# Two aggregations of a graph network kernel: gathers released by the product itself, index columns copied six at a time

## The chip, the core and the metric

One core of a Trainium2 chip runs the whole program. TensorE (PE in the rows) multiplies matrices, and its weight loads stand apart as PEld; VectorE (DVE), ScalarE (ACT) and GpSimd (POOL) work element by element, and SyncE (SP) starts plain transfers. Each engine runs its own instruction stream in order. They meet through semaphores: an instruction adds to a counter when it is done, another engine's instruction waits until the counter has reached a number. A gather (rows of a table in the chip's main memory, picked by a column of indices) is a DMA that GpSimd prepares and starts; its rows land later and count up a semaphore of their own.

The metric is the device time of one execution in microseconds (us), the median of several runs.

## The reference

Four layers follow one another, each with a residual: a graph attention layer, a mixture of eight experts, a graph convolution with edge weights, and a mixture of four experts whose routing is itself a small graph attention. The change touches the two edge aggregations over the same 53125 edges and 3125 nodes, of 256 values each:

```python
# layer 0: softmax over the edges of each destination node
m = jax.ops.segment_max(a, dst, num_segments=N)
a = jnp.exp(a - m[dst])
denom = jax.ops.segment_sum(a, dst, num_segments=N)
a = a / (denom[dst] + 1e-16)
out = relu(jax.ops.segment_sum(h[src] * a[:, None], dst, num_segments=N))
# layer 2: weighted sum
gathered = A_values[:, None] * h[col]
agg = jax.ops.segment_sum(gathered, row, num_segments=A_shape)
```

## The kernel before

Nodes lie in 25 tiles of 128 (`NT`). The edges, sorted by destination, lie in columns of 128; six columns (`BG`) are a block, and the blocks of a tile are its edges. `emit_aggregate` is called twice: with tag `a0` and `softmax` true for the attention layer (its blocks start where the tile's edges start), and with tag `a1` for the convolution, where every tile's blocks are padded and lie one behind another. The number of blocks is read at run time; in this data there are 77 in `a0` (462 gathers) and 74 in `a1` (444 gathers), some three a tile.

For every column of a block four things happen:

1. ScalarE copies one column of source indices into one of six places of `idx` (`put_indices`, L572 to L574).
2. GpSimd gathers 128 rows of 260 values by them into one of six places of `rows` (L589).
3. A matrix of weights `w` (128 edges by 128 nodes, zero where edge and node don't belong together) is made: in `a0` by ScalarE as an exponential of a mask `nb` (L789), in `a1` by VectorE (L658).
4. TensorE multiplies `w` by `rows` and adds to the tile's sum in PSUM (L619). One product is two matrix instructions in the trace, since the data is float32.

The semaphore `agg_done` counts these products; PE starts it at `BG` = 6. ScalarE's copy of column i of block g waits until it reaches `g * BG + i + 1`, that is, until the product that used the same place one block earlier is done. The copy adds one to `indexed`, and the gather waits for that count. So the place in `rows` is guarded through ScalarE: product, copy, gather. In `a0` ScalarE's stream is, for each block, six copies, a wait for the mask (`masked`), and six exponentials; between tiles it reads the next tile's range (L780 to L783). In `a1` it has the copies alone.

VectorE in `a0` walks the tiles in a loop of 22 turns (the other three tiles stand before and behind it): copy the negated maxima (`keep_max`, L716), mask the first block (L722, L726), negate the next tile's maxima (L708 to L712), mask the other blocks, finish the previous tile (`finish_tile`, L734 to L740), and scan the tile two ahead for its maxima (`scan`: six masks L684 and six maxima L701 a block). The masks `nb` go into a ring of four blocks, so VectorE may run ahead of ScalarE and TensorE. In `a1` VectorE makes `w` and evicts each tile's sum (L661); at a tile's end TensorE closes the sum with a product of zeros (L623) and opens the next with another (L612).

Of the kernel before, what the change touches and what calls it, by code (L numbers as in the profile page):

```python
# [15 lines left out]
P = 128  # L16
# [486 lines left out]
def emit_aggregate(nc, S, tag, table, softmax):  # L503
# [9 lines left out]
    with ExitStack() as ctx:  # L513
        sb = lambda n, s, d: ctx.enter_context(nc.sbuf_tensor(tag + n, s, d))
        idx = sb("idx", [P, BG], I32)
# [55 lines left out]
        def put_indices(act, g, c):  # L571
            for i in range(BG):  # L572
                act.wait_ge(agg_done, g * BG + i + 1)
                nc.scalar.copy(idx[:, i:i + 1], source[:, bass.ds(c + i, 1)]).then_inc(indexed, 1)  # L574

        @block.gpsimd
        def _(pool):
            if softmax:
                total = tile_range(nc, pool, S, NT - 1)[0]
            else:  # L580
                total = pool.value_load(S.eranges[0:1, NT:NT + 1], min_val=1, max_val=EBLOCKS)
            count = pool.alloc_register(tag + "_count")
            pool.reg_mov(count, 0)
            with pool.Fori(0, total) as g:
                for i in range(BG):
                    pool.reg_add(count, count, 1)
                    pool.wait_ge(indexed, 1)
                    pool.wait_ge(indexed, count)
                    pool.indirect_dma_start(rows[:, i, 0:TW], None, table,  # L589
                                            bass.IndirectOffsetOnAxis(ap=idx[:, i:i + 1], axis=0)).then_inc(gathered[i], 16)  # L590

        @block.tensor
        def _(pe):
            pe.sem_inc(agg_done, BG)
# [50 lines left out]
        if not softmax:  # L645
            @block.vector
            def _(v):
# [3 lines left out]
                with v.Fori(0, NT) as t:  # L651
                    tiles.load(t)
                    tiles.step()
                    with tiles.blocks() as g:
                        c = tiles.chunk(g)
                        for i in range(BG):
                            v.wait_ge(agg_done, g * BG + i + 1)
                            nc.vector.tensor_scalar(w[:, i, :], S.iota[:, 0:P], S.elane[:, bass.ds(c + i, 1)],  # L658
                                                    S.eweight[:, bass.ds(c + i, 1)], ALU.is_equal, ALU.mult).then_inc(weighed, 1)
# [5 lines left out]
            def _(act):  # L665
                total = act.value_load(S.eranges[0:1, NT:NT + 1], min_val=1, max_val=EBLOCKS)
                with act.Fori(0, total) as g:
                    put_indices(act, g, slot_of(nc, act, g, EBLOCKS, BG))
            return
# [106 lines left out]
        def _(act):  # L776
# [3 lines left out]
            with act.Fori(0, NT) as t:  # L780
                tiles.load(t)
                tiles.step()
                with tiles.blocks() as g:  # L783
# [3 lines left out]
                    for i in range(BG):  # L787
                        act.wait_ge(agg_done, g * BG + i + 1)
                        nc.scalar.activation(w[:, i, :], nb[:, bass.ds(g % RING, 1), i, :].rearrange("p a n -> p (a n)"), ACT.Exp, bias=S.score[:, bass.ds(c + i, 1)]).then_inc(weighed, 1)  # L789

# [1050 lines left out]
```

## Time and profile before

| | before |
|---|---|
| median of 3 runs | 3885.39 us |
| lowest and highest | 3881.91 and 3893.16 us |
| the profiled execution | 3854.0 us |
| its span, first to last instruction | 3851.9 us |
| mean granted TensorE clock over the span | 0.712 |
| PE, PEld busy | 2660.5 us (69%), 1816.4 us (47%) |
| DVE, ACT, POOL busy | 1510.2 us (39%), 759.3 us (20%), 1889.8 us (49%) |
| first aggregation (`a0`), from first index copy to last sum | 704 to 1515 us |
| second aggregation (`a1`) | 2452 to 3112 us |

The table and the rows below come from one profiled execution. Busy time is that of the instructions themselves: a wait, a register instruction or the flight of a DMA is not in it. A row of a timeline has the start, the length, the engine, the line, the operation with what it writes and reads, the number of instructions merged into it, and in brackets how long the engine had been idle and what the profile takes for the releaser. "issue" there means that no semaphore ended the idle time: the engine's own sequencer was late.

### The profile page before, as it was taken

How to read it: one execution, taken by the hardware profiler on the slowest of the kernel's cores; microseconds unless marked ns; L12 is line 12 of the kernel's file. 1: busy time of each engine (PE TensorE's matmuls, PEld its weight loads, DVE VectorE, ACT ScalarE, POOL GpSimd, SP SyncE). 2: the span in 40 equal slices, each digit the busy share in tenths (PEclk: the TensorE clock that was granted, in tenths of full speed). 3: DMA queues.
4: the chain of work that ended last, by engine and by line, in shares of the span. 5: the costliest groups of instructions: out<-in, count | busy, mean ns of one | idle time of the engine just before them, and what ended most of it. 6: DMA issues, size and time to landing. Idle time of an engine off the chain costs nothing. (4 is left out here: it accounts for less than half of the span.)

```text
span 3851.9 us, 46754 instructions
## 1 busy us (share of the span) xinstructions
PE 2660.5 (69%) x10550; PEld 1816.4 (47%) x10551; DVE 1510.2 (39%) x3666; ACT 759.3 (20%) x2605; POOL 1889.8 (49%) x1926
## 2 busy tenths in 40 slices
PE   3249688465566556699999997677777755989900
PEld 2225587233333333576767665333333334666600
DVE  5774555656666653322222223322222233000075
ACT  0136000123322222222222221111111112222200
POOL 0000666265656554366666663366666611666602
PEclk9555555566666665799999998666666665999955
DMA  2012344132222222100000000233333311110001
GB/s 73 27 38 66 143 146 147 33 83 75 79 79 79 74 76 61 33 11 12 12 12 12 14 1 20 77 91 91 91 89 92 89 26 34 20 20 8 9 36 36
DMA packets 124782, 213.24 MB, mean 55 GB/s; under 512 B 56098, under 2 KB 82807, under 8 KB 122423
## 3 DMA queue, kind: packets, MB, share of 16 engines
q0 software_dynamic: 75808, 125.28, 13.1%
q1 hardware_dynamic: 48918, 87.37, 6.7%
q8 instruction: 18, 0.29, 0.0%
q14 instruction: 38, 0.30, 0.0%
HBM read 196.99 MB, written 15.52 MB: 55 GB/s over the span
## 5 line engine op out<-in xcount | busy, mean ns | idle before, releaser
L589 POOL DMA_INDIRECT a0rows<-table,a0idx x462 | 466.3, 1009 | 363.0 <-ACT a0idx L574 250.5
L589 POOL DMA_INDIRECT a1rows<-table,a1idx x444 | 420.1, 946 | 315.3 <-ACT a1idx L574 176.6
L619 PE MATMUL a1ps<-a1rows,a1w 128*128 128x256 f32 x888 | 435.5, 616 | 173.2 <-DMA a1rows<-table,a1idx 115.9
L619 PE MATMUL a0ps<-a0rows,a0w 128*128 128x257 f32 x924 | 428.3, 602 | 153.6 <-ACT a0w L789 71.4
L1053 POOL DMA_INDIRECT erecords<-k_rece x416 | 404.5, 972 | 213.3 <-issue 103.2
L881 PE MATMUL f0up<-k_xnT,f0w 128*128 x1280 | 386.0, 457 | 59.4 <-ACT f0hid L913 33.7
L1053 POOL DMA_INDIRECT records<-k_recg x288 | 301.0, 1045 | 226.1 <-POOLq L959 74.2
L1373 POOL DMA_INDIRECT gt_land<-table_gat,gt_source x281 | 265.9, 946 | 287.7 <-DVEq L1402 141.7
L619 PEld LDWEIGHTS a1ps<-a1rows,a1w 128*128 128x128 f32 x888 | 215.5, 284 | 393.2 <-issue 278.2
L619 PEld LDWEIGHTS a0ps<-a0rows,a0w 128*128 128x128 f32 x924 | 233.5, 286 | 345.8 <-issue 176.6
L891 PE MATMUL f0dn<-f0w,f0hid 128*128 128x256 f32 x1600 | 357.6, 380 | 9.2 <-issue 8.6
L881 PEld LDWEIGHTS f0up<-k_xnT,f0w 128*128 128x128 f32 x1280 | 246.5, 199 | 193.3 <-issue 57.7
L891 PEld LDWEIGHTS f0dn<-f0w,f0hid 128*128 128x128 f32 x1600 | 304.1, 190 | 56.2 <-issue 14.6
L832 DVE SCALAR_TENSOR_TENSOR k_x<-f0dn,k_gate,k_x 128x256 f32 (+1 forms) x200 | 88.9, 479 | 507.5 <-PE f0dn L891 330.1
L913 ACT ACTIVATE f0hid<-f0up,f0b1now 128x384 f32<-128x384 f32 (+1 forms) x320 | 167.7, 528 | 539.8 <-PE f0up L881 327.8
L658 DVE TENSOR_SCALAR a1w<-k_iota,k_elane,k_eweight 128x128 f32<-128x128 f32 x444 | 148.1, 370 | 266.1 <-PE a1ps L619 149.5
L1610 PE MATMUL f1dn<-gt_arena 128*128 128x256 f32 x800 | 191.0, 388 | 28.6 <-issue 24.3
L1600 PE MATMUL f1up<-k_xnT,gt_arena 128*128 x640 | 187.5, 449 | 23.5 <-DVE gt_arena L1417 14.1
L574 ACT COPY a1idx<-k_esource 128x1 int32 x444 | 82.7, 191 | 578.5 <-PE a1ps L619 351.8
L789 ACT ACTIVATE a0w<-a0nb,k_score 128x128 f32 x462 | 143.7, 389 | 235.1 <-DVE a0nb L726 183.0
L471 PEld LDWEIGHTS es_ps<-k_we_attn,es_ea 128*128 128x128 f32 x832 | 182.1, 332 | 5.6 <-issue 5.3
L1610 PEld LDWEIGHTS f1dn<-gt_arena 128*128 128x128 f32 x800 | 152.8, 193 | 62.1 <-issue 42.3
(387 smaller groups left out, 3133.3 us busy)
## 6 DMA issues: line engine op xcount, KB each, us to landing
es_ea<-in_eaT SPq DMA_DIRECT2D x16, 1664.0 KB
es_lane<-lane_row SPq DMA_DIRECT2D x16, 832.0 KB
so_rowl<-glane_row SPq DMA_DIRECT2D x32, 256.0 KB
a0rows<-table,a0idx POOLq DMA_INDIRECT x462
a1rows<-table,a1idx POOLq DMA_INDIRECT x444
erecords<-k_rece POOLq DMA_INDIRECT x416
table<-k_tbl SPq DMA_DIRECT2D x10, 650.0 KB, 3.6
records<-k_recg POOLq DMA_INDIRECT x288
```

The costliest lines, as they stand in the source:

```text
L471: nc.tensor.matmul(ps[i][:, 2, c:c + 1], ea[:, i, c * P:(c + 1) * P], S.we_attn[:, 0:1], start=True, stop=True).then_inc(step, 1)
L589: pool.indirect_dma_start(rows[:, i, 0:TW], None, table, bass.IndirectOffsetOnAxis(ap=idx[:, i:i + 1], axis=0)).then_inc(gathered[i], 16)
L619: nc.tensor.matmul(sum_of(t), w[:, i, :], rows[:, i, 0:width], start=False, stop=False).then_inc(agg_done, 1)
L658: nc.vector.tensor_scalar(w[:, i, :], S.iota[:, 0:P], S.elane[:, bass.ds(c + i, 1)], S.eweight[:, bass.ds(c + i, 1)], ALU.is_equal, ALU.mu ...
L789: nc.scalar.activation(w[:, i, :], nb[:, bass.ds(g % RING, 1), i, :].rearrange("p a n -> p (a n)"), ACT.Exp, bias=S.score[:, bass.ds(c + i ...
L881: ins = nc.tensor.matmul(up[q % 2][:, 0:size], w1[:, k, m * P:(m + 1) * P], S.xnT[:, k, bass.ds(g * (U * P) + a * P, size)], start=(k == 0 ...
L891: ins = nc.tensor.matmul(down[j][:, 0:D], hid[half][:, k, (j - a) * P:(j - a + 1) * P], w2[:, k, :], start=(k == 0), stop=(k == KH - 1))
L913: nc.scalar.activation(hid[half][:, m, :], up[q % 2][:, 0:(b - a) * P], ACT.Gelu, bias=bias_now[:, m:m + 1]).then_inc(hid_ready, 1)
L1053: pool.indirect_dma_start(self.rec_dram, bass.IndirectOffsetOnAxis(ap=self.rec[:, c + 1, 0:1], axis=0), self.rec[:, c + 1, 1:R], None).the ...
L1373: pool.indirect_dma_start(land[:, j, :], None, S.table_gat, bass.IndirectOffsetOnAxis(ap=source[:, j:j + 1], axis=0)).then_inc(gathered[la ...
L1600: ins = nc.tensor.matmul(up[q % 2][:, 0:size], w1[:, k, m * P:(m + 1) * P], S.xnT[:, k, bass.ds(g * (U * P) + a * P, size)], start=(k == 0 ...
L1610: ins = nc.tensor.matmul(down[j][:, 0:D], hid[half][:, k, (j - a) * P:(j - a + 1) * P], w2[:, k, :], start=(k == 0), stop=(k == KH - 1))
```

## The change

The copy takes six index columns in one instruction and puts them into one of two places, by the parity of the block. It waits until `agg_done` reaches `g * BG + 1`; since the counter is now started at `BG + 1`, this means that all products of block g - 2 are done, whose gathers used the same place. `indexed` now counts blocks. The gather waits once a block for the index columns, and for each column for `agg_done` itself. GpSimd's loop goes in pairs of blocks, so that each half has its place of `idx` written in; with an odd number of blocks six gathers too many are made at the end, whose rows nobody uses, and a wait behind the loop lets all gathers land. ScalarE adds one to `indexed` at its end, for that last half pair. The waits of `w` are the same as before, written with the new start of the counter.

```diff
-        idx = sb("idx", [P, BG], I32)
+        idx = sb("idx", [P, 2 * BG], I32)
...
         def put_indices(act, g, c):
-            for i in range(BG):
-                act.wait_ge(agg_done, g * BG + i + 1)
-                nc.scalar.copy(idx[:, i:i + 1], source[:, bass.ds(c + i, 1)]).then_inc(indexed, 1)
+            act.wait_ge(agg_done, g * BG + 1)
+            nc.scalar.copy(idx[:, bass.ds(g % 2 * BG, BG)], source[:, bass.ds(c, BG)]).then_inc(indexed, 1)
...
-            count = pool.alloc_register(tag + "_count")
-            pool.reg_mov(count, 0)
-            with pool.Fori(0, total) as g:
+            pairs = pool.snap((pool.snap(total) + 1) // 2)
+            count, block_count = pool.alloc_register(tag + "_count"), pool.alloc_register(tag + "_blocks")
+            pool.reg_mov(count, 1)
+            pool.reg_mov(block_count, 0)
+
+            def gather_block(half):
+                pool.reg_add(block_count, block_count, 1)
+                pool.wait_ge(indexed, 1)
+                pool.wait_ge(indexed, block_count)
                 for i in range(BG):
                     pool.reg_add(count, count, 1)
-                    pool.wait_ge(indexed, 1)
-                    pool.wait_ge(indexed, count)
+                    pool.wait_ge(agg_done, 1)
+                    pool.wait_ge(agg_done, count)
                     pool.indirect_dma_start(rows[:, i, 0:TW], None, table,
-                                            bass.IndirectOffsetOnAxis(ap=idx[:, i:i + 1], axis=0)).then_inc(gathered[i], 16)
+                                            bass.IndirectOffsetOnAxis(ap=idx[:, half * BG + i:half * BG + i + 1], axis=0)
+                                            ).then_inc(gathered[i], 16)
+
+            with pool.Fori(0, pairs):
+                for half in range(2):
+                    gather_block(half)
+            landed = pool.snap(pairs * 32)
+            for i in range(BG):
+                pool.wait_ge(gathered[i], 16)
+                pool.wait_ge(gathered[i], landed)
...
-            pe.sem_inc(agg_done, BG)
+            pe.sem_inc(agg_done, BG + 1)
...
-                            v.wait_ge(agg_done, g * BG + i + 1)
+                            v.wait_ge(agg_done, g * BG + i + 2)
...
-                        act.wait_ge(agg_done, g * BG + i + 1)
+                        act.wait_ge(agg_done, g * BG + i + 2)
```

On ScalarE, in the loop of the second aggregation, the names are the index places (`a1idx`) and the source columns of the padded blocks (`k_esource`). Before, a turn of the loop was:

```order
L574 ISA
L574 COPY a1idx<-k_esource 128x1
L573 REGISTER_ALU
L574 ISA
L574 COPY a1idx<-k_esource 128x1
L573 REGISTER_ALU
```

and so on, six copies in all. Now the whole turn is:

```order
L681 ISA
L573 ISA
L573 COPY a1idx<-k_esource 128x6
L681 REGISTER_ALU
L681 COMPARE_AND_BRANCH
```

Five copies of six with their waits and counters are gone, and nothing else stands there. In the first aggregation the six exponentials, which stood behind the sixth copy of their block, now stand behind the one copy.

On GpSimd, in the loop of the second aggregation, the gather writes `a1rows` from `table`. Before, a block was six times this pair:

```order
L584 UNCONDITIONAL_BRANCH
L586 REGISTER_ALU
L589 DMA a1rows<-table,a1idx 128x260
L586 REGISTER_ALU
L589 DMA a1rows<-table,a1idx 128x260
```

Now the first gather of a block has one more counter ahead of it:

```order
L598 UNCONDITIONAL_BRANCH
L587 REGISTER_ALU
L591 REGISTER_ALU
L594 DMA a1rows<-table,a1idx 128x260
L591 REGISTER_ALU
L594 DMA a1rows<-table,a1idx 128x260
```

The turn has twelve gathers in place of six, and one register instruction more for each block.

## Rows read from the trace of the kernel before

**Rows 1.** The page's groups: line, engine, operation, count, busy us, mean ns, idle before.

```profile
L589 POOL DMA_INDIRECT a0rows<-table,a0idx x462 | 466.3, 1009 | 363.0 <-ACT a0idx L574 250.5
L589 POOL DMA_INDIRECT a1rows<-table,a1idx x444 | 420.1, 946 | 315.3 <-ACT a1idx L574 176.6
```

**Rows 2.** Busy time by stretch, one per aggregation: PE, PEld, DVE, ACT, POOL, clock, DMA.

```profile
704.00:1516.00 812.00, 492.52 (x1099) 269.91 (x1099) 473.58 (x1328) 228.28 (x924) 466.26 (x462) 0.62 0.28 76
2451.00:3112.00 661.00, 485.22 (x988) 243.81 (x988) 158.66 (x469) 82.69 (x444) 420.15 (x444) 0.61 0.33 90
```

**Rows 3.** Waits of VectorE, 740 to 1500 us: total us, times, longest.

```profile
DVE a0mb L684 <- issue: 102.6, 141, 4.7
DVE a0top L701 <- issue: 52.2, 60, 2.5
```

**Rows 4.** Waits of GpSimd, 740 to 1500 us.

```profile
POOL a0rows L589 <- ACT a0idx L574: 197.1, 102, 8.8
POOL a0rows L589 <- issue: 109.5, 348, 1.8
```

**Rows 5.** Waits of GpSimd, 2455 to 3105 us.

```profile
POOL a1rows L589 <- issue: 138.7, 382, 2.7
POOL a1rows L589 <- ACT a1idx L574: 92.6, 61, 3.6
```

**Rows 6.** Timeline of one tile of the first aggregation.

```profile
1026.59 0.99 POOL L589 DMA_INDIRECT a0rows<-table,a0idx  x1 [0.30 <-ACT a0idx L574]
...
1030.63 1.26 DVE L684 TENSOR_SCALAR a0mb<-k_iota,k_dstf 128x128 f32 x6 [0.51 <-issue]
...
1034.62 0.19 ACT L574 COPY a0idx<-k_src 128x1 int32 x1 [1.58 <-issue]
1034.68 0.90 DVE L684 TENSOR_SCALAR a0mb<-k_iota,k_dstf 128x128 f32 x4 [0.73 <-issue]
...
1037.95 0.95 POOL L589 DMA_INDIRECT a0rows<-table,a0idx  x1 [0.30 <-issue]
...
1040.74 1.64 DVE L701 SCALAR_TENSOR_TENSOR a0top<-a0mb,k_score,a0top 128x128 f32<-128x128 f32 x5 [1.05 <-issue]
...
1041.02 1.08 ACT L574 COPY a0idx<-k_src 128x1 int32 x6 [4.23 <-PE a0ps L619]
...
1041.98 0.95 POOL L589 DMA_INDIRECT a0rows<-table,a0idx  x1 [3.08 <-ACT a0idx L574]
...
1043.08 1.27 DVE L684 TENSOR_SCALAR a0mb<-k_iota,k_dstf 128x128 f32 x6 [0.70 <-issue]
```

**Rows 7.** Timeline around two restarts of the gathers, second aggregation.

```profile
2470.62 0.94 POOL L589 DMA_INDIRECT a1rows<-table,a1idx  x1 [0.30 <-issue]
...
2474.25 0.52 ACT L574 COPY a1idx<-k_esource 128x1 int32 x3 [4.71 <-PE a1ps L619]
2474.30 0.95 DVE L658 TENSOR_SCALAR a1w<-k_iota,k_elane,k_eweight 128x128 f32<-128x128 f32 x3 [4.55 <-PE a1ps L619]
...
2475.21 0.94 POOL L589 DMA_INDIRECT a1rows<-table,a1idx  x1 [3.65 <-ACT a1idx L574]
...
2478.09 2.46 PE L619 MATMUL a1ps<-a1rows,a1w 128*128 128x256 f32 x4 [3.95 <-DMA a1rows<-table,a1idx]
...
2719.18 1.21 PE L619 MATMUL a1ps<-a1rows,a1w 128*128 128x256 f32 x2 [0.75 <-issue]
...
2720.50 0.19 ACT L574 COPY a1idx<-k_esource 128x1 int32 x1 [1.78 <-PE a1ps L619]
...
2725.14 0.19 ACT L574 COPY a1idx<-k_esource 128x1 int32 x1 [4.44 <-PE a1ps L619]
...
2726.20 0.94 POOL L589 DMA_INDIRECT a1rows<-table,a1idx  x1 [2.19 <-issue]
```

**Rows 8.** Timeline of the end of the first aggregation.

```profile
1474.12 1.57 POOL L589 DMA_INDIRECT a0rows<-table,a0idx  x1 [2.15 <-ACT a0idx L574]
...
1492.10 0.94 POOL L589 DMA_INDIRECT a0rows<-table,a0idx  x1 [2.32 <-ACT a0idx L574]
...
1505.84 0.94 POOL L589 DMA_INDIRECT a0rows<-table,a0idx  x1 [0.30 <-issue]
...
1509.57 2.55 PE L619 MATMUL a0ps<-a0rows,a0w 128*128 128x257 f32 x4 [0.48 <-DMA a0rows<-table,a0idx]
...
1514.35 0.42 DVE L740 TENSOR_TENSOR k_x<-k_x,a0relu 128x256 f32<-128x256 f32 x1
```

More of the change, by code:

```diff
@@ L668, in _ @@
                     put_indices(act, g, slot_of(nc, act, g, EBLOCKS, BG))
+                act.drain().then_inc(indexed, 1)
             return
@@ L787, in _ @@
                     for i in range(BG):
-                        act.wait_ge(agg_done, g * BG + i + 1)
+                        act.wait_ge(agg_done, g * BG + i + 2)
                         nc.scalar.activation(w[:, i, :], nb[:, bass.ds(g % RING, 1), i, :].rearrange("p a n -> p (a n)"), ACT.Exp, bias=S.score[:, bass.ds(c + i, 1)]).then_inc(weighed, 1)
+            act.drain().then_inc(indexed, 1)
 def wait_for_event(pool, event, up_done, down_done):
```

## The prediction

> **What bounds the kernel now.** I read the page's costliest groups first, then the waits of each engine inside the two aggregations, then their timelines. The groups [rows 1] say where the change acts: 462 and 444 gathers on GpSimd, both told to wait mostly for ScalarE's index copy. By stretch [rows 2] the first aggregation takes 812 us and the second 661 us of a span of 3851.9 us; GpSimd is busy for 466 and 420 us of them. The rest of the kernel is not touched, so all that can be won or lost lies in these 1473 us.
>
> The pitch of gathers in an unbroken run is 0.95 us plus 0.30 us between two, 1.25 us [rows 6, 7]. At that pitch 444 gathers take 555 us; the second aggregation takes 106 us more, and nearly all of that is idle time of GpSimd. Its waits [rows 5] are 138.7 + 92.6 = 231.3 us; 443 gaps of 0.30 us are 133 of them, so 98 us are real stops, and 61 stops are put down to the index copy. Here the gathers are in a closed loop: gather, its landing (2.88 us from the start of the gather at 2475.21 to the product at 2478.09 [rows 7]), product, release of the place six gathers back, gather.
>
> The first aggregation is another case. Its VectorE shows in the loop no wait for another engine, only "issue" [rows 3]: it goes from scan to mask to scan without a pause, about 30.5 us a tile, and the masks and maxima of the other engines hang on it. GpSimd's 197.1 us of waiting there [rows 4] is mostly waiting for work that VectorE has not made possible yet. Where VectorE's turn is longer than the gathers' (some 18 a tile, 23 us), a faster release of gathers gives nothing.
>
> **The restart of a gather.** Today a finished product is seen by ScalarE, which copies, and by GpSimd after that. At 2719.18 a product runs 1.21 us and ends at 2720.39; the copy starts at 2720.50, a hop of 0.11 us; the copy lasts 0.19 us. At the stop after a tile's end the copy starts at 2725.14 and the gather at 2726.20, 1.06 us later [rows 7]. Without ScalarE between them the copy's 0.19 us and one hop of 0.11 us go: 0.30 us a restart. The bounds are 0 (if the copy was not what came last) and 1.06 us (all from copy to gather). I take 0.30, since the other 0.76 us lie on GpSimd after its wait and stay.
>
> Second aggregation: 61 stops by 0.30 us is 18.3 us. In unbroken runs a release comes early enough already and nothing changes. Many of the stops are not short ones: at 2474.25 ScalarE and at 2474.30 VectorE, which wait for the same counter of products, go on together after 4.71 and 4.55 us of idle [rows 7]. The counter itself came late, not the copy. GpSimd, waiting for the counter itself, gets it no sooner; it saves the 0.30 us there and not the 3.65 us. That is why I don't count the 98 us as the gain.
>
> **The copies.** Five of six are gone, some 385 and 370 of them by 0.19 us. In the second aggregation ScalarE has nothing else to do: no gain beyond the restart. In the first one the exponentials of a block stand behind its sixth copy, which waits for the last product of the block before (copy at 1034.62 [rows 6]). They can now start product by product. That moves the last block's products of a tile about 1 us forward (the landing of its first gather decides in place of the copies), and the next tile's first product still waits for VectorE's mask: 0 us in the loop, as long as VectorE is the bound.
>
> **The tail of the first aggregation.** After VectorE's last mask the chain is gathers and products. Two stops of GpSimd there, 2.15 us at 1474.12 and 2.32 us at 1492.10 [rows 8], come from copies queued behind exponentials; less the usual 0.30 us they are 1.85 + 2.02 us. The last gather starts at 1505.84; by 2.88 us to its product, and 1.23 us for one (2.46 us for two at 2478.09 [rows 7]), the end would be at 1509.95, where the last products end at 1509.57 + 2.55 = 1512.12: 2.17 us. The most is 6.0 us, the least 2 restarts, 0.6 us; I take 4.
>
> **What is added.** 77 blocks are odd, so the first aggregation makes six gathers more, each after the last block's product in its place. The last of them starts some 0.8 us after the last product and lands 2.88 us later (3.7 us), while VectorE's finish ends at 1514.35 + 0.42, 2.65 us after it [rows 8]: 1 us more. 74 blocks are even: nothing there. GpSimd's extra counter and wait a block have no row of their own. At best they hide behind the gather that is running, as the present pair does. At worst they lengthen the gap once a block, by one more 0.30 us: 151 blocks, 45 us. I take 0, because the present gap is the same 0.30 us with a counter and two waits between any two gathers, however early they were released [rows 6, 7]. The six-column copy replaces 0.19 us by something near 0.19 us, a block ahead of need.
>
> **The sum.** 18.3 + 4 - 1 = 21 us. The profiled execution takes 3854.0 us and would take 3833. The timed median is 31.4 us above the profiled one; I carry the difference over: 3885.4 - 21 = 3864 us. The own range of this case is 3846 to 3874.
>
> **A stall that may grow or shrink.** In the first aggregation the scan of a tile's second block starts at 1034.68 and the third's at 1043.08, 8.40 us, where the first took 1034.68 - 1030.63 = 4.05 us for the same instructions [rows 6]. These 4.35 us, once a tile, fall into the last part of an unbroken run of ten gathers (1026.59 to 1037.95 and its landing) and end when the run has ended; the six gathers from 1041.98 have none beside them. The 102.6 + 52.2 us of "issue" [rows 3] hold this. I take it as a stall of VectorE's (and ScalarE's) sequencer under a long run of gathers, and don't know its cause.
>
> By the Trainium skill (NOTIFIC — the notification-queue block, section 7.1) the recording of traces always pushes back on the engines when its inner queue fills, so these stalls could be those of the recording. Then timed runs would not have them and both of the next two rivals would be void. But they would then have to be faster than the profiled one, and the three timed runs are 31 us slower; no run here settles it. The sum would be the same by either.
>
> **Rivals.**
> First, slower: the runs join. The tile's first six gathers now start 3.08 us after the last ended [rows 6], released by six copies in one row at 1041.02. If ScalarE gets through its tile change before the stall begins, they follow at 0.30 us, the run becomes 16 or more, and the third block's scan is stalled like the second: 4.35 us in up to 22 turns, 96 us on the bounding engine, less the 21: 3960 us, and 3912 for half of the turns. It turns the result slower than before by more than 0.3% from 8 turns on (33 us by 4.35). For it: the stall follows the length of a run. Against: ScalarE is stalled by the same thing (4.23 us idle ahead of 1041.02), and the counter of products comes late in it, so the run would still break.
>
> Second, much faster: the stalls grow rarer, since five copies of six with their waits, counters and increments leave the engines that are stalled. Half of 22 by 4.35 us, and half of the 98 us of stops: 97 us, 3788 us. For it: the index copies are 462 of ScalarE's 924 instructions there [rows 1, 2]. Against: VectorE's and TensorE's instructions stay, and so do the gathers.
>
> Third, no gain: the second aggregation is held by TensorE. At the lower clock a product takes 1.23 us [rows 7], hardly less than the pitch of 1.25, and the clock is 0.61 on the mean there [rows 2], so mostly 1.2 GHz; 444 products and 50 products of zeros at 1.23 us would be 608 us of the 661. Gathers that start earlier would then wait as landed rows. Only the tail is left, 3 us: 3882 us.
>
> Fourth, slower: the added wait is not hidden, 45 us less 21: 3909 us. Behind it on GpSimd stands the next gather, and behind that the product.
>
> **The chances.** Forecast 0.45, joined runs 0.14, rarer stalls 0.15, TensorE the bound 0.20, the added wait 0.06. No change means within 0.3%, 11.7 us, about what this measurement can tell. Faster: nearly all of the forecast (0.42), all of the rarer stalls, a little of the third (0.02): 0.59. Slower: the first and the fourth: 0.20. The same: 0.21. The range over all cases, 3800 to 3905, leaves out the full joining and the far end of the rarer stalls.
>
> **What would show it.** Right: in the second aggregation GpSimd's stops of over 0.30 us are as many as before and some 0.3 us shorter, released by TensorE; the stretch is some 18 us shorter; the stall of the second scan stays at 4 us; VectorE's turn stays at 30.5 us; the first stretch is 3 us shorter. Joined runs: no stop ahead of a tile's first gather and a long third scan. Rarer stalls: a second scan of 4 us, and a shorter turn. TensorE: stops shorter but landed gathers waiting, the second stretch unchanged. The added wait: a gap over 0.30 us ahead of every sixth gather. The forecast is wrong if the first stretch moves by over 10 us either way.

## The result, and the profile after

The kernel became slower: 3999.1 us (median of 4 runs, 3989.2 to 4010.1), where the kernel before took 3887.9 (4 runs). The ratio is 1.0287, with a 95% interval of 1.0256 to 1.0319: 111 us more, where 21 less were forecast. The profiled execution of after took 3989.2 us, its span is 3987.1. The two traces differ by more than the timed runs do, by 135 us: 98 and 10 of them lie in the two aggregations, and 27 in stages where the kernels are alike (935.0 and 948.5 us between the aggregations, 739.9 and 753.1 behind the second).

By stretch (us, PE, PEld, DVE, ACT and POOL busy, clock, DMA share, GB/s), one row per aggregation:

```profile
704.00:1614.50 910.50, 533.11 (x1099) 268.26 (x1099) 478.12 (x1328) 175.25 (x539) 470.46 (x468) 0.58 0.26 68
2563.00:3234.00 671.00, 458.45 (x988) 238.02 (x988) 160.06 (x469) 14.55 (x74) 422.31 (x444) 0.64 0.33 88
```

Against [rows 2] the first aggregation took 98 us more and the second 10 us more. VectorE's busy time is nearly the same (473.6 and 478.1 us): it does not do more, it stands still more. ScalarE has fewer instructions (539 for 924), as the change says. The page's groups of gathers answer to [rows 1]:

```profile
L594 POOL DMA_INDIRECT a0rows<-table,a0idx x468 | 470.5, 1005 | 464.4 <-PE a0ps L633 260.6
L594 POOL DMA_INDIRECT a1rows<-table,a1idx x444 | 422.3, 951 | 324.5 <-PE a1ps L633 101.8
```

The waits of VectorE and GpSimd between 740 and 1600 us (total us, times, longest) answer to [rows 3, 4]:

```profile
DVE a0top L716 <- issue: 140.2, 122, 3.2
DVE a0mb L699 <- issue: 111.0, 146, 4.6
...
POOL a0rows L594 <- PE a0ps L633: 234.7, 115, 13.3
POOL a0rows L594 <- issue: 90.3, 295, 0.5
```

The idle "issue" time of VectorE's masks and maxima went from 102.6 + 52.2 = 154.8 us to 251.2 us: 96 us more, nearly the whole loss of this stretch. GpSimd has only small gaps left (longest "issue" 0.5 us, before 1.8), and long waits for a product in their place.

One tile shows how. It is the timeline of after; the times in brackets are the idle time before the instruction:

```profile
1025.32 1.40 POOL L594 DMA_INDIRECT a0rows<-table,a0idx  x1 [9.33 <-PE a0ps L633]
1027.02 1.34 POOL L594 DMA_INDIRECT a0rows<-table,a0idx  x1 [0.30 <-PE a0ps L633]
...
1028.67 0.98 POOL L594 DMA_INDIRECT a0rows<-table,a0idx  x1 [0.30 <-ACT a0idx L573]
...
1032.71 1.27 DVE L699 TENSOR_SCALAR a0mb<-k_iota,k_dstf 128x128 f32 x6 [0.51 <-issue]
...
1036.76 0.29 DVE L699 TENSOR_SCALAR a0mb<-k_iota,k_dstf 128x128 f32 x1 [0.73 <-issue]
...
1037.89 0.20 ACT L573 COPY a0idx<-k_src  x1 [1.29 <-issue]
...
1040.08 0.31 DVE L699 TENSOR_SCALAR a0mb<-k_iota,k_dstf 128x128 f32 x1 [1.08 <-issue]
...
1041.38 0.95 POOL L594 DMA_INDIRECT a0rows<-table,a0idx  x1 [0.30 <-issue]
...
1043.62 0.35 DVE L716 SCALAR_TENSOR_TENSOR a0top<-a0mb,k_score,a0top 128x128 f32<-128x128 f32 x1 [2.50 <-issue]
...
1045.14 1.06 POOL L594 DMA_INDIRECT a0rows<-table,a0idx  x1 [0.31 <-issue]
...
1049.26 0.97 POOL L594 DMA_INDIRECT a0rows<-table,a0idx  x1 [3.06 <-remote]
...
1050.11 1.42 DVE L699 TENSOR_SCALAR a0mb<-k_iota,k_dstf 128x128 f32 x6 [0.70 <-issue]
...
1060.81 1.40 POOL L594 DMA_INDIRECT a0rows<-table,a0idx  x1 [9.33 <-PE a0ps L633]
```

Fourteen gathers follow each other at 1.25 us, from 1028.67 to 1045.14, where before there were ten up to a pause of 3.08 us [rows 6]. Two slower gathers (1.70 and 1.65 us from start to start) stand straight ahead of them, and two such ahead of the ten in before: counted by the gap of 0.30 us, the unbroken run is 16 in place of 12, and the second run of a turn is 2 in place of 6. The run ends at 1046.20 because GpSimd itself waits then, for 3.06 us, for a product that had ended by 1044.25: it sees the count late too. The second scan block starts at 1036.76 and the third at 1050.11: 13.35 us, where before it was 8.40 and a block without a stall takes 4.05. The third block is not stalled, since the run has ended by then. From gather to gather the turn is 35.49 us (1025.32 to 1060.81), 5.0 us over the 30.5 of before. The products of the stretch start from 736.2 to 1610.2 in after (874.0 us), and from 736.0 to 1511.5 in before (775.5).

In the second aggregation the hurt place is the change of tile. First before, then after: the tile's last product, the closing product, VectorE's finish, the next tile's first product.

```profile
2850.07 1.22 PE L619 MATMUL a1ps<-a1rows,a1w 128*128 128x256 f32 x2 [0.98 <-DMA a1rows<-table,a1idx]
2851.22 1.22 PE L623 MATMUL a1ps<-k_iota,k_zeros 1*128 1x256 f32 x2
2852.75 0.42 DVE L661 TENSOR_TENSOR k_agg<-a1ps,k_bias_row 128x256 f32 x1 [9.25 <-issue]
2854.81 5.03 PE L619 MATMUL a1ps<-a1rows,a1w 128*128 128x256 f32 x12 [1.52 <-DVE a1w L658]
```

```profile
2861.69 1.21 PE L633 MATMUL a1ps<-a1rows,a1w 128*128 128x256 f32 x2 [0.73 <-DMA a1rows<-table,a1idx]
2862.84 1.22 PE L637 MATMUL a1ps<-k_iota,k_zeros 1*128 1x256 f32 x2
2867.34 0.42 DVE L675 TENSOR_TENSOR k_agg<-a1ps,k_bias_row 128x256 f32 x1 [12.00 <-DMA erecords<-k_rece]
2869.30 4.12 PE L633 MATMUL a1ps<-a1rows,a1w 128*128 128x256 f32 x9 [4.39 <-DVE a1w L672]
```

From the end of the last product to the next tile's first it is 3.5 us in before and 6.4 in after. Over all 24 changes the mean is 3.5 us in before and 5.2 in after, 40 us more in all; from the first to the last product the aggregation takes 653.4 and 663.6 us. VectorE starts 3.28 us after the closing product has ended (2864.06 to 2867.34); in before 0.31 us. The unbroken run of gathers reaches up to the change now.

### The profile page after: what moved, and what is told of

Read it like the earlier page. It is cut to its first block and busy times, and to the rows that moved or that the text cites. A ratio compares the mean times of both kernels' runs of the same rounds, so it can differ in the third digit from the quotient of the medians.

```text
span 3987.1 us, 45141 instructions
## 1 busy us (share of the span) xinstructions
PE 2672.2 (67%) x10550; PEld 1810.4 (45%) x10551; DVE 1520.2 (38%) x3666; ACT 637.7 (16%) x1850; POOL 1898.4 (48%) x1932
## 5 line engine op out<-in xcount | busy, mean ns | idle before, releaser
L633 PE MATMUL a1ps<-a1rows,a1w 128*128 128x256 f32 x888 | 408.1, 584 | 210.5 <-DMA a1rows<-table,a1idx 115.3
L633 PE MATMUL a0ps<-a0rows,a0w 128*128 128x257 f32 x924 | 456.4, 619 | 128.8 <-DMA a0rows<-table,a0idx 72.0
L804 ACT ACTIVATE a0w<-a0nb,k_score 128x128 f32 x462 | 162.6, 395 | 676.8 <-DVE a0nb L741 479.7
L716 DVE SCALAR_TENSOR_TENSOR a0top<-a0mb,k_score,a0top 128x128 f32<-128x128 f32 x462 | 140.4, 349 | 153.2 <-issue 140.5
L471 PE MATMUL es_ps<-k_we_attn,es_ea 128*128 128x1 f32 x832 | 177.7, 349 | 1.2 <-issue 1.2
```

Of the source, the lines that this page charges most:

```text
L471: nc.tensor.matmul(ps[i][:, 2, c:c + 1], ea[:, i, c * P:(c + 1) * P], S.we_attn[:, 0:1], start=True, stop=True).then_inc(step, 1)
L633: nc.tensor.matmul(sum_of(t), w[:, i, :], rows[:, i, 0:width], start=False, stop=False).then_inc(agg_done, 1)
```

## Experiments

The kernel before was run beside each group, on five chips: 3859 us (e1 to e4), 3860 (e5, e5b, c1, c2), 3854 (e6, e7, c3, c4), 3915 (e8, e9, e10, c5) and 3904 (e12, c7); ratios are to its runs on the same chip, and times and stretches of different chips compare only roughly. "Stretch" is from the start of the first product to the start of the last in the first aggregation of the profiled execution (before: 775.5 us, after: 874.0); "stall" is the idle "issue" time of VectorE's masks and maxima in one window, 740 to 1430 us (before 149.0, after 208.4; about 43 to 49 of it are there without any stall, as e3 and c4 show; a faster kernel has more turns in this window).

| kernel | first aggregation | ratio or time | stretch | stall |
|---|---|---|---|---|
| e1 | as before; second changed | 1.0056 (1.0037 to 1.0076) | | |
| e2 | changed; second as before | 1.0247 (1.0222 to 1.0272) | 868.1 | 205.2 |
| e3 | e2, wait for 6 of 6 | 1.0316 (1.0291 to 1.0342) | 888.0 | 42.9 |
| e5b | e2, wait for 5 of 6 | 1.0032 (1.0016 to 1.0048) | 782.2 | 47.9 |
| e5 | e2, wait for 4 of 6 | 0.9820 (0.9795 to 0.9845) | 700.8 | 56.5 |
| e12 | e5, another chip | 0.9931 (0.9900 to 0.9961) | 741.3 | 82.1 |
| e10 | e2, wait for 3 of 6 | 1.0195 (1.0168 to 1.0221) | 867.9 | 201.7 |
| e7 | before, wait for 4 of 6 | 0.9857 (0.9842 to 0.9872) | 709.7 | 63.4 |
| e8 | e2, ScalarE between | 1.0029 (1.0010 to 1.0047) | 795.5 | 149.1 |
| c1 | e2, 64 rows | 3966.6 us, one run | 868.6 | 210.0 |
| c2 | e2, 256 bytes a row | 3954.4 us, one run | 874.6 | 211.8 |
| c3 | e2, 17 columns | 3971.0 us, one run | 870.3 | 205.0 |
| c5 | e2, fixed columns | 3916.3 us, one run | 798.3 | 166.9 |
| c4 | e2, memsets | 3717.9 us, one run | 630.7 | 49.2 |
| c7 | e2, plain DMAs | 3748.7 us, one run | 638.0 | 49.2 |

**Where the loss is.** In e1 the change is made where `softmax` is false, in e2 where it is true; the other aggregation is as before:

```diff
+        direct = not softmax        # e1;  e2: direct = softmax
```

> The change in the second aggregation alone; the first as before. Theory (the loss is in the first aggregation, the second gains nothing: its gathers run from the first to the last start in 660.7 us after and 650.4 us before, by the two traces): 3898 us, between 3885 and 3905, ratio 1.000 to 1.005. Rival (the 18 us of the prediction are there in timed runs, and the profiled execution of before was a lucky one): 3870 us, ratio 0.995. Rival (the second aggregation carries a good part of the 111 us): over 3920 us.

> The change in the first aggregation alone; the second as before. Theory (joined runs: 14 gathers without a pause in place of 10, VectorE's stall lasts about 10 us a tile in place of 4 to 5, its turn 35.5 us in place of 30.5; the stretch grows by 98 us): 3985 us, between 3970 and 3995, ratio 1.022 to 1.027. Rival (the loss comes only when both are changed, or lies outside of the two): under 3930 us.

Measured: 22 us and 95 us, together 117, where after costs 111. e2 is inside its range; e1 is just above its own, whose theory gave the second aggregation no loss of more than 0.5%. In e1's trace the change of tile takes 6.0 us on the mean over 24 tiles, 60 us more than before in all; 21 of these stay (674.6 us from the first to the last product, before 653.4), so the rest of the aggregation is some 40 us shorter. So the forecast's gain in the second aggregation is turned into a loss, and the place of the loss fits the same cause: the run of gathers reaches up to the change.

**Breaking the runs.** e3, e5b, e5 and e10 have one wait more ahead of each block's first gather, for all, five, four or three products of the block before:

```diff
                 pool.wait_ge(indexed, block_count)
+                pool.reg_add(begin, count, 6)       # e5b: 5, e5: 4, e10: 3
+                pool.wait_ge(agg_done, 1)
+                pool.wait_ge(agg_done, begin)
```

> e2 with one wait more on GpSimd ahead of each block's first gather: all six products of the block before. So no run is longer than six gathers; who waits for what is otherwise as in e2. Theory (VectorE's stall follows the length of a run): no scan block over 4.5 us beside gathers, but each block has a pause of 2.5 to 3 us on GpSimd (2.93 us from a gather's start to its product, 0.70 to 1.2 us for it, less the pitch of 1.25): the gathers' turn of three blocks is 30 to 31 us, as long as before's turn: 3885 us, between 3865 and 3910. Rival (the stall comes from GpSimd waiting for the same counter as VectorE and ScalarE, whatever the length of a run): the stalls stay, and the pauses come on top: 4000 us or more.

e3's stall is gone (42.9 us), which speaks for the run's length and against the shared counter. The time alone would not tell it: 3977 us is outside the theory's range and near the rival's 4000. The size was wrong: the pause is 4.1 us, not 2.5 to 3, and 35 us a turn are now the gathers' own. From e3's timeline, and below it from the waits of its VectorE, 740 to 1600 us:

```profile
939.99 0.94 POOL L616 DMA_INDIRECT a0rows<-table,a0idx  x1 [4.11 <-PE a0ps L655]
...
951.63 0.95 POOL L616 DMA_INDIRECT a0rows<-table,a0idx  x1 [4.13 <-PE a0ps L655]
```

```profile
DVE a0m L746 <- PE a0psT L638: 216.6, 23, 17.2
DVE a0mb L722 <- issue: 45.5, 71, 0.7
```

VectorE, which had no wait for another engine before [rows 3], now waits 216.6 us for TensorE's maxima, 9.4 us a tile: without a stall its turn is 35.0 - 9.4 = 25.6 us. This is the number that was missing in the prediction: of before's 30.5 us, 4.9 were stall.

> As e3 (the first aggregation changed, the second as before), but the wait ahead of a block's first gather asks for four of the six products of the block before, not all six: the pause of 4.1 us that e3 has ahead of each block becomes 4.1 - 2 x 1.25 = 1.6 us. VectorE's turn without a stall is 25.6 us (35.0 us a turn in e3, of which it waits 9.4 us for TensorE's maxima). Theory (a short break is enough to keep the stall away): blocks of gathers at 6.25 + 0.95 + 1.6 = 8.8 us, a turn of 26.5 to 27.5 us in place of before's 30.5: 65 to 85 us less than before, 3775 to 3800 us (before: 3859). Rival (it needs the full pause, what fills up drains too slowly): the stall of 5 to 10 us a tile comes back, 3930 to 3990 us.

> As e5, with five of six products: a pause of 2.9 us. If the short break of e5 is enough, this one costs 1.25 us more a block: turns of 30.2 us, 3850 to 3875 us, and no stall. If e5's is not enough and this one is, then 3850 to 3875 us where e5 stays over 3930.

Both as the theory said: 3787.5 and 3871.3 us. A break of 1.6 us is enough there, and e5 beats both kernels. One turn's gathers in e5's timeline have breaks of 1.5 to 1.6 us and no long ones:

```profile
976.32 0.94 POOL L616 DMA_INDIRECT a0rows<-table,a0idx  x1 [1.53 <-issue]
976.70 1.26 DVE L722 TENSOR_SCALAR a0mb<-k_iota,k_dstf 128x128 f32 x6 [0.73 <-issue]
...
980.72 1.28 DVE L722 TENSOR_SCALAR a0mb<-k_iota,k_dstf 128x128 f32 x6 [0.70 <-issue]
...
985.20 0.95 POOL L616 DMA_INDIRECT a0rows<-table,a0idx  x1 [1.52 <-issue]
```

> As e5 (first aggregation alone), but the wait ahead of a block's first gather asks for three of six products: a pause of 0.35 us where e5 has 1.6 us. If even the shortest break lets the stall go, the gathers' turn is under VectorE's 25.6 us and this is the fastest: 3760 to 3780 us, ratio 0.975 to 0.980. If the break has to be longer (as e6 shows for the second aggregation, where runs of 16 stayed), runs of 16 and stalls of 10 us a tile: 1.02 to 1.03. I expect the second.

The ratio and the stall are as expected, the runs are not quite. The wait mostly leaves 0.3 to 0.4 us ahead of a tile's second block, which is hardly more than the usual gap, and 1.6 to 2.4 us ahead of its third. Most long runs are of twelve, as in before, and yet the stall is e2's. In before the pause behind the twelve is over 3 us and the stall ends in it; here the gathers go on after 1.61 us, while VectorE is stalled, and it stays so:

```profile
979.80 0.95 POOL L616 DMA_INDIRECT a0rows<-table,a0idx  x1 [1.61 <-PE a0ps L655]
...
986.21 0.48 DVE L722 TENSOR_SCALAR a0mb<-k_iota,k_dstf 128x128 f32 x2 [3.98 <-issue]
```

So a break of 1.6 us every six gathers mostly keeps a stall away (e5), and one of 1.6 us doesn't end a stall that has begun. No kernel here has a break of between 0.4 and 1.5 us ahead of every block.

> e5 once more, on another chip. In e9, on a chip where the kernel before takes 3915 us in place of 3859, the same first aggregation had stalls again in the profiled execution (its stretch 796 us, e5's and e6's 701) and the runs spread over 67 us. Theory (the gain of e5 holds on the chip where it was measured and is smaller where the break is just too short): between 0.980 and 0.998, with a larger spread than before's. If the gain is a matter of the kernel alone: 0.9795 to 0.9845 again.

The theory's side. The gain is there, but smaller, and the runs spread from 3836 to 3906 us (before: 3890 to 3912); the profiled one, with a span of 3867, has 82.1 us of stall. So 1.6 us is at the edge: how much of the stall stays away differs from chip to chip or run to run.

> The kernel before, with nothing changed but the same wait on GpSimd ahead of each block's first gather in the first aggregation (four of the six products of the block before). Theory (all of e5's gain comes from breaking the runs, none from the change itself): within 0.3% of e5, ratio to before 0.979 to 0.986. Rival (the shorter release of the gathers pays once the stall is away): e5 is faster than this by 15 us or more, this at 0.986 or over.

```diff
             with pool.Fori(0, total) as g:
+                if softmax:
+                    pool.reg_add(begin, count, 4)
+                    pool.wait_ge(agg_done, 1)
+                    pool.wait_ge(agg_done, begin)
```

Nearly all of the gain comes without the change. The two stretches differ by 9 us in favour of e5 and the ratios by 0.4%, but they were taken on two chips and e12 lies on the other side: whether the shorter release pays once the stall is away stays open.

**Which part joins the runs.** In e8 ScalarE raises a count product by product, and the gathers wait for it as well:

```diff
+            for i in range(BG):
+                act.wait_ge(agg_done, g * BG + i + 2)
+                act.sem_inc(token, 1)
...
                     pool.wait_ge(agg_done, count)
+                    pool.reg_add(tokens, tokens, 1)
+                    pool.wait_ge(token, 1)
+                    pool.wait_ge(token, tokens)
```

> e2, but each gather of the first aggregation waits for a count of ScalarE's as well, which ScalarE raises product by product in the row where its copies stood before (one copy of six columns, then six waits for a product with an increment each, then the exponentials). So the change's other parts stay and ScalarE stands between product and gather again. Theory (the loss comes from GpSimd no longer passing through ScalarE, which is stalled too and so breaks the runs): runs of ten and six as before, VectorE's turn 30.5 us, ratio to before 0.997 to 1.004. Rival (the joined runs come from the early index copy or the exponentials that start early): runs of 14 and 1.02 or over, as e2.

The theory holds: 1.0029, and the stall is 149.1 us as in before (149.0). By the trace 22 of the runs are of twelve again, each up to a pause of some 3.7 us, in which GpSimd waits for ScalarE's count. The early copy and the double place cost little (the interval is 0.1 to 0.5%). What costs is that GpSimd doesn't wait for the stalled ScalarE any more.

**The second aggregation.**

```diff
+                pool.reg_add(begin, count, 4 if softmax else 3)   # e6;  e9: 4 in both
```

> Both aggregations changed, each with a wait for some of the products of the block before ahead of a block's first gather: four of six in the first (as e5), three of six in the second, which costs it 4.1 - 3 x 1.25 = 0.35 us a block. Theory (in the second aggregation the stall sits on the change of tile: from a tile's last product to the next tile's first 3.4 us in the trace of before, 6.4 us in that of e1, over 24 tiles 85 and 144 us; the break keeps it away): the tile change is back at 3.4 us, a turn of 18 gathers takes 25.5 to 26 us in place of before's 26.9: 20 to 35 us under e5, ratio to before 0.973 to 0.977. Rival (0.35 us is too short a break for the stall to stay away): the tile change stays over 5 us and the second aggregation at e1's length: 15 to 25 us over e5, ratio 0.986 to 0.989.

> Both aggregations changed and both with the wait of e5 (four of six products). The first is e5's. In the second, theory: blocks at 8.8 us by 74 are 651 us, as long as before's 650 us, and the change of tile at 3.4 to 4 us; but a block whose wait meets a change of tile is late by as much: 0 to 25 us over e5, ratio 0.981 to 0.989. Rival (as in e6 the wait moves the gathers behind the change of tile and long runs follow): the second aggregation as in e6, ratio 1.00 to 1.01.

e6 was wrong beyond its rival: 1.0071, 96 us over e5. Its second aggregation takes 749.8 us from the first to the last product. A block whose wait meets a change of tile starts late, the rest of the tile follows in one run of 16, and this ends in the next change:

```profile
2604.47 0.94 POOL L598 DMA_INDIRECT a1rows<-table,a1idx  x1 [4.45 <-PE a1ps L637]
...
2622.04 1.21 PE L637 MATMUL a1ps<-a1rows,a1w 128*128 128x256 f32 x2 [0.92 <-DMA a1rows<-table,a1idx]
...
2629.49 0.42 DVE L679 TENSOR_TENSOR k_agg<-a1ps,k_bias_row 128x256 f32 x1 [14.01 <-DMA erecords<-k_rece]
2631.04 1.65 DVE L676 TENSOR_SCALAR a1w<-k_iota,k_elane,k_eweight 128x128 f32<-128x128 f32 x6 [1.12 <-issue]
2631.44 4.83 PE L637 MATMUL a1ps<-a1rows,a1w 128*128 128x256 f32 x12 [6.19 <-DVE a1w L676]
```

The change takes 8.2 us here. e9 came out at 1.0011 (0.9978 to 1.0043), which its rival had (1.00 to 1.01) and its theory not. Its trace isn't read here; and as the gain in the first aggregation differs from chip to chip (e12), the time alone doesn't say what the second aggregation loses in e9.

**What the stall needs.** e4 was to make the pitch longer, with a memset and a drain ahead of every gather:

```diff
+                    nc.gpsimd.memset(pad[:, 0:32], 0.0)
+                    pool.drain()
```

> e2 with a small memset (128 x 32) and a drain on GpSimd ahead of every gather: runs as long as in e2, but at a pitch of some 1.6 us in place of 1.25. Theory A (the stall needs a number of gathers in a row and a rate above what something drains; at the lower rate nothing fills): stalls shorter than 2 us a tile, VectorE's turn 27 to 30 us, gathers' turn 18 by 1.6 = 29 us: 3870 us, between 3850 and 3900. Theory B (it follows the number of gathers in a row or their time alone): stalls of 10 us as in e2, 3985 to 4020 us.

Neither theory's pitch was reached: a memset of 0.14 us and a drain after a gather cost far more than thought, the pitch became 3.57 us (ratio 1.2364), with 2.5 us of idle time before each gather. At that pitch there is no stall: the idle "issue" time ahead of VectorE's masks is 45.5 us over the whole aggregation and never over 0.7 us. So theory B, the number of gathers in a row or their time alone, is out, unless the 2.5 us between any two count as breaks; theory A isn't tested between a pitch of 1.25 and 3.57 us.

```profile
1041.92 0.95 POOL L615 DMA_INDIRECT a0rows<-table,a0idx  x1 [2.49 <-issue]
1042.87 0.14 POOL L613 MEMSET a0pad<- 128x32 f32 x1
...
1045.49 0.95 POOL L615 DMA_INDIRECT a0rows<-table,a0idx  x1 [2.48 <-issue]
```

Six kernels change what a gather or its neighbours do, and leave out a part of the work or do another in its place, so they don't compute the reference:

```diff
-  pool.indirect_dma_start(rows[:, i, 0:TW], None, table, ...
+  pool.indirect_dma_start(rows[0:64, i, 0:TW], None, table, ...     # c1
+  pool.indirect_dma_start(rows[:, i, 0:64], None, table, ...        # c2
+  nc.gpsimd.memset(rows[:, i, 0:TW], 1.0)                           # c4
+  pool.dma_start(rows[:, i, 0:TW], table[0:P, :])                   # c7
...
-  nc.tensor.matmul(sum_of(t), w[:, i, :], rows[:, i, 0:width],
+  nc.tensor.matmul(<last 17 columns of the sum>, w[:, i, :], rows[:, i, 240:257],   # c3
...
-  mask(mb, t, c, i)                     and S.score[:, bass.ds(c + i, 1)]
+  <the same with S.dstf[:, i:i + 1]>    and S.score[:, i:i + 1]      # c5
```

> e2 with gathers in the first aggregation that fetch 64 rows in place of 128 (the other half of each place holds ones, set once at the start). Theory (something that each row of a gather adds to fills up over a run): the stalls vanish or begin twice as late, after 16 gathers, and VectorE's turn is 26 to 28 us where e2 has 35.2: 3790 to 3830 us. Rival (it hangs on the number of gathers, or the time of an unbroken run): stalls of about 10 us a tile as in e2, 3950 us.

> e2 with gathers in the first aggregation that fetch 256 bytes a row in place of 1040 (the rest of each place holds ones, set once at the start). If the stall comes from the bytes moved, it vanishes: 3790 to 3830 us. If it comes from the number of rows, descriptors or transfers, it stays as in e2, about 10 us a tile: 3950 us. I expect it to stay.

> e2 with products in the first aggregation of 17 columns in place of 257 (the other columns of the sum stay zero): TensorE has as many instructions but far less work, and its products leave the lower clock. If the stall comes from TensorE's work (its clock, its load), it vanishes: 3860 us or less. If it hangs on the gathers' run, the stalls of about 10 us a tile stay: 3940 to 3960 us. I expect them to stay.

> e2 with each gather of the first aggregation replaced by a memset of the same 260 columns on GpSimd, with the same waits and counts: no DMA, and the products are no longer paced by gathers but by TensorE (about 1.23 us each). Theory (the stall needs the gathers): no stall, VectorE's turn 25.6 us as in e3 less its waits: the stretch some 700 us or less, 3740 to 3800 us. Rival (it comes from the long unbroken run of products and their counters): VectorE's masks and maxima are still stretched to blocks of 8 us.

> e2 with each gather of the first aggregation replaced by a plain DMA of 128 rows of the table, from GpSimd's queue, into the same place, with the same waits and counts (the rows are fixed ones). If the stall needs GpSimd's work on an indirect gather, it vanishes and the time is c4's, 3720 to 3800 us. If it comes from the transfers that GpSimd starts at this pace, it stays: 3930 to 3990 us. By c1 and c2, where half the rows and a quarter of the bytes changed nothing, I expect the first.

> e2 with scans in the first aggregation whose 12 instructions a block read fixed columns (of destination and score) in place of columns named by a register; the maxima start at 60. So VectorE has no register work between them. Theory (what is stalled is the sequencer's register work, some 0.7 us each): the scan blocks under a gather run lose most of the stall, the turn is 27 to 30 us in place of 35.2, 3830 to 3880 us. Rival (everything that VectorE starts is late, whatever its operands): turn and time as in e2, 3950 us.

Half the rows, a quarter of the bytes and products of a fraction of the size change nothing: stall and stretch are e2's. (c3's forecast that its products would leave the lower clock did not come true: the granted clock is 0.50 in its first aggregation, 0.58 in e2's. Its TensorE is busy for 344 us there in place of 536. So c3 tests TensorE's load and not its clock.) The theory of c1 (rows fill something up) is refuted. Without the indirect gather, by a memset (c4) or by a plain DMA of the same 130 KB from the same queue (c7, 0.54 us on GpSimd where a gather takes 0.95), the stall is gone and VectorE's own pace is left, 26 us a turn. In both, GpSimd is busy for a smaller part of the time too and its runs are shorter (6 to 12 in c7, at 0.60 us from one to the next), so they don't part the indirect form from GpSimd's long unbroken work. c5 has half of an answer: the masks run at full pace inside a block, but one idle time of over 6 us takes the place of many small ones.

```profile
951.08 1.27 DVE L722 TENSOR_SCALAR a0mb<-k_iota,k_dstf 128x128 f32<-128x128 f32 x6 [1.53 <-issue]
...
958.68 1.83 DVE L738 SCALAR_TENSOR_TENSOR a0top<-a0mb,k_score,a0top 128x128 f32<-128x128 f32 x6 [6.33 <-issue]
```

So it is not the register work alone. The stretch is 70 us shorter than e2's (798.3 and 868.1), but that is no measure of the stall: a scan block without one takes 3.56 us here (from 942.82 to 946.38) and 4.05 in the others, which over 77 blocks is 38 of the 70 us, and c5 ran on another chip than e2.

What in the chip makes the stall stays open.

## Why the prediction was wrong

**The failed step** is the weighing of the first rival: "Against: ScalarE is stalled by the same thing [...], so the run would still break." It broke, but four gathers later (by the gap of 0.30 us the prediction's run of ten is one of twelve, and after's is one of 16). In before the stalled ScalarE copied late, and that ended the run after ten gathers. With GpSimd waiting for the product itself the run goes on to fourteen, and each gather more prolongs the stall by its 1.25 us: 4 x 1.25 = 5.0 us a tile, which is just the turn's growth from 30.5 to 35.5 us. e8 shows that taking ScalarE from between is the cause, and e3, e5 and e5b that breaking the runs takes the stall away.

**The sentence that led there** was "In unbroken runs a release comes early enough already and nothing changes", and with it "0 us in the loop". The loop of the first aggregation was held by VectorE, as read. But VectorE was held in part by the gathers, and an earlier gather was not free. The rival's price, 4.35 us in up to 22 turns, was nearly right (96 us; measured 95 in e2); its place was not: the second block is stalled for longer, the third is not stalled. It had a chance of 0.14, and its number of 3960 us still took off the 21 us of gain.

**The second aggregation.** The term of 18.3 us came out at 22 us of loss (e1). The restarts did move to TensorE, but the sign that the prediction named, as many stops and each 0.3 us shorter, isn't there: GpSimd stands idle for over 0.35 us 59 times in before and 68 times in after, for 97 and 105 us beyond the usual gap. The change of tile is longer, too. Fewer stops to save was not the matter; the prediction had seen that the counter comes late in a stall and drew from it only that nothing is gained.

**The small terms.** The added counter and wait cost nothing, as taken: in after the gap at a block's turn is 0.30 us, as between any two (1041.38 in the timeline is a block's first gather). The 4 us of the tail are not there: from the end of VectorE's last mask to the end of the last product it is 34.4 us in before, 35.8 in after and 35.5 in e2, with stops of 2.04 and 2.63 us on GpSimd in after in place of the 2.15 and 2.32 us of before. The six gathers more were not measured by themselves. The second rival, rarer stalls from fewer instructions, is refuted by after itself: ScalarE has 539 for 924 there, and the stall is longer. The third, TensorE as the bound of the second aggregation, was not tried by itself; what the runs show there is time above such a floor, at the changes of tile.

**The recording.** The prediction named the Trainium skill (NOTIFIC — the notification-queue block, section 7.1) as a way in which the stalls could be those of the recording. The timed runs of after are as slow as its profiled one (3999 and 3989 us). But each of them lists a granted clock, so none here was surely made without a recording. Against it speaks c7: over its first aggregation the trace has as many instructions as e2's (1099 on TensorE, 1328 and 1327 on VectorE, 468 on GpSimd) and 92 GB/s in place of 69, all in 674 us in place of 904, and no stall. So a higher mean rate of what is recorded doesn't bring the stall; a backlog that only the indirect gathers make is not excluded, and the question stays open. A second page is worth a look: by the Trainium skill (SBUF — State Buffer, "Who interferes with whom") only VectorE and GpSimd share a port, and ScalarE waits on nobody. The trace does not agree with this as the whole cause, since ScalarE stops at the same time: its copy at 2867.17 and VectorE's finish at 2867.34 come together, both over 3 us after the closing product had ended (2864.06).

```profile
2867.17 0.20 ACT L573 COPY a1idx<-k_esource  x1 [12.16 <-DMA records<-k_recg]
```

## What to carry to other kernels

An engine that shows only "issue" idle time is not yet at its own pace: look which other engine's unbroken run lies beside the long gaps, and cut that run once (one wait more) before anything is made faster. A slow middleman between two engines can be what spaces their work; where it is taken out, ask what will now run without a pause and who stands beside it. Here a wait that was added, and nothing removed, was worth 1.4% (e7), and the change of the first aggregation with it 1.8% (e5), 0.7% on another chip (e12).

## What the hardware showed unexpectedly

- With more than about eight indirect gathers in a row at a pitch of 1.25 us (VectorE's first long gap mostly begins 9 to 10 us into the run, the two slower gathers ahead not counted, and its last mostly ends 1 to 4 us after the run), VectorE and ScalarE issue late and counts of products are seen late. Runs of six with breaks of 4.1 or 2.8 us have none of it; breaks of 1.6 us have some.
- It doesn't depend on rows, bytes or TensorE's load in that time (c1 to c3). And it isn't tied to these two loops, whose counts are in registers: in another stage of before, on line L1373, whose gathers stand in straight code, fourteen follow at the same pitch. For the first 7 us of the run ScalarE's activations are on time. The last one starts at 3306.66, 5.1 us after the product that it waits for, the last of L1600, has ended (3301.53). VectorE's additions start at 3312.66, all five in a row, when the products of three of them had ended by 3306.71:

```profile
3292.47 0.94 POOL L1373 DMA_INDIRECT gt_land<-table_gat,gt_source  x1 [3.01 <-remote]
3292.68 8.85 PE L1600 MATMUL f1up<-k_xnT,gt_arena 128*128 x32
...
3299.85 0.47 ACT L1576 ACTIVATE gt_arena<-f1up,gt_b1now 128x256 f32<-128x256 f32 x1 [0.46 <-issue]
...
3301.37 5.34 PE L1610 MATMUL f1dn<-gt_arena 128*128 128x256 f32 x24
...
3306.66 0.47 ACT L1576 ACTIVATE gt_arena<-f1up,gt_b1now 128x256 f32<-128x256 f32 x1 [3.75 <-remote]
...
3308.70 0.94 POOL L1373 DMA_INDIRECT gt_land<-table_gat,gt_source  x1 [0.30 <-issue]
...
3312.66 1.97 DVE L1412 TENSOR_TENSOR gt_y<-f1dn,gt_b 128x256 f32 x5 [18.84 <-remote]
```

- A memset of 0.14 us and a drain on GpSimd between two gathers made the pitch 3.57 us, 2.3 us more than without (e4).
